# A two-layer mixture-of-experts kernel: the experts' output bias moves from 8-row products into VectorE's gated product, and the adapter step's operands are zero-filled to 128 rows

## The chip, the cores and the metric

The kernel runs on one core of a Trainium2 chip. The metric is the device time in microseconds; smaller is better. The engines are called by the names of the profile: PE is TensorE's products, PEld its weight loads, DVE is VectorE, ACT ScalarE, POOL GpSimd, and SP the engine that issues most DMAs. A name with a q behind it (SPq) is an engine's queue.

## The reference, cut to what matters

```python
# layer 0: 8 experts over all 2048 tokens, every expert weighted by a gate (many gates are zero)
h = gelu_tanh(einsum('bld,ehd->bleh', x, w1) + b1)
y = einsum('bleh,edh->blde', h, w2) + b2.T            # b2: one vector of 128 per expert
out = einsum('blde,ble->bld', y, gates)
# layer 1: an adapter per sample, chosen by its language id, then a norm ...
h = relu(einsum('bsh,bha->bsa', x, W1[lang]) + b1[lang])
adapted = einsum('bsa,bah->bsh', h, W2[lang]) + b2[lang]
x1 = layernorm(x + adapted) * gamma[lang] + beta[lang]
# ... and 8 experts, of which each token takes two
out_e = einsum('eblh,ehd->ebld', gelu(einsum('bld,edh->eblh', layernorm(x1), w1) + b1), w2) + b2[:, None, None, :]
x = x + einsum('ble,ebld->bld', cw, out_e) + x1
```

There are N = 2048 tokens of width 128, in four groups g of 512. An expert has 512 hidden units, in four chunks of 128.

## The kernel before

**Tiling.** A "dense unit" is one expert's chunk of 128 hidden units for one group of 512 tokens. On PE it takes three products for the first matrix (L573 to L575, a high and a low part of each operand), a Gelu on ACT (L643), and one f32 product for the second matrix (L620), which the profile counts as two. Four units make a step: one expert's output y for one group. There are 32 steps in layer 0. Then come 19 "tiles" of 256 sorted tokens (layer 1 for groups 0 to 2, L550 to L552 and L612 to L614), and last 8 dense steps for group 3 of layer 1.

**Order.** Nothing is scheduled while the program runs. Every piece of work is put into its engine's queue by `at(engine, position, function)`, and the positions are in units of PE's dense work. The table `AT` holds the distances of the small work, and `HURRY` holds those for group 2. An engine runs its queue strictly in this order and waits on semaphores.

**Sums.** Each y is multiplied by its gate row, copied to all 128 partitions (Gs, loaded by SP at L762), on DVE into a ring of three buffers tmp (`gated`, L709). POOL adds tmp into acc (`add`, L738). Terms that do not need a gate are copied from PE's bank to tmp by ACT (`copied`, L725). `terms` lists all of them in order. The first 12 steps of layer 0 are finished before the gates are known, so ACT keeps their y in SBUF (L688).

**Output bias.** The sum over experts of gate times b2 is a product with 8 rows (the experts): `b2_mm`, L1219, with b2f (8x128) as weights and gTb (8x2048, the gates by expert) as the moving operand, one product for each group of layer 0 and one for group 3 of layer 1. For groups 0 to 2 of layer 1 the same product opens the bank in which the sorted results come together (`moe`, L1756), and 128-row products L1760 follow it.

**Adapter step.** `mid(g)` runs once for each group, when the sum of layer 0 for it is complete. Its first PE work is `pe_h` (L1237); ACT writes the relu to hTs, whose row 33 is all ones for the bias. Then `pe_xa` does, for each of four blocks of 128 tokens, a product with the identity (L1258: x itself) and one with hTs and cw2 (L1259: 32 rows and the bias row) into the same bank. DVE takes its statistics (L1267), and the norm, the logits (L1371), the choice of experts and, for groups 0 to 2, the scatter of the tokens into sorted order (POOL, L1637) follow. The tiles can't start before the last of these scatters.

**Bank ring.** Small products share PSUM banks 6 and 7; a plan by position (`misc`) gives each its bank and the semaphore that it waits for.

Of the kernel before, what the change touches and what calls it, by code (L numbers as in the profile page):

```python
# [12 lines left out]
ALU = mybir.AluOpType  # L13
# [5 lines left out]
NG = 4  # L19
# [110 lines left out]
def build_adaln_ffn(nc, t, out):  # L130
# [19 lines left out]
    with ExitStack() as ctx:  # L150
# [65 lines left out]
        b2f = [sb(f"b2f{i}", [E, D]) for i in range(2)]  # L216
# [53 lines left out]
        cw2 = sb("cw2", [A + 1, B, D])  # L270
        fgb = sb("fgb", [D, 2])
        hTs = sb("hTs", [A + 1, 512])
# [67 lines left out]
        s_gtb = [sem(f"s_gtb{i}") for i in range(1 + NG)]  # L340
# [26 lines left out]
        b_b2 = sem("b_b2")  # L367
# [88 lines left out]
        def group_of(kind, v):  # L456
            return STEPS[v][2] if kind == "y" else (v if kind in ("x2", "moe") else v[1])

        def layer_of(kind, v):
            return STEPS[v][0] if kind == "y" else (1 if kind in ("x2", "moe") else v[0])  # L460
# [21 lines left out]
        for g in range(NG):  # L482
            misc.append((4 * ND + 6 + 5 * g + 0.35, ("b2", (0, g)), in_tmp(where[("b2", (0, g))])))
# [15 lines left out]
        misc.append((UD + 8.35, ("b2", (1, 3)), in_tmp(where[("b2", (1, 3))])))  # L499
# [195 lines left out]
        def gated(i, v):  # L695
            def fn(dve):
# [12 lines left out]
                dve.tensor_tensor(o, src, Gs[:, j % NGS, :], ALU.mult).then_inc(s_tmp, 1)  # L709
            return fn  # L710

        def copied(i, kind, v):
            def fn(act):
                if i >= NTMP:
                    act.wait_ge(s_acc, i - NTMP + 1)
                if kind == "b2":
                    act.wait_ge(b_b2, [("b2", x) for _, k, x in terms if k == "b2"].index(("b2", v)) + 1)
                    src = bank[mb[("b2", v)][0]]
                elif kind == "moe":
# [186 lines left out]
        def sp_later(sp):  # L906
            sp.dma_start(b2f[0][:, :], t["b2_0"]).then_inc(load_sem("b2f0"), 16)
            sp.dma_start(b2f[1][:, :], t["b2_1"]).then_inc(load_sem("b2f1"), 16)
# [13 lines left out]
            sp.wait_ge(p_no, B)  # L922
            for b in range(B):
# [3 lines left out]
                sp.dma_start(cw2[:, b, :], t["cw2"][bass.ds(r, 1), :, :].rearrange("a p c -> p (a c)")).then_inc(s0, 16)  # L927
# [281 lines left out]

        b2_order = [v for _, k, v in terms if k == "b2"]  # L1210

        def b2_mm(v):
# [704 lines left out]
```

## Time and profile before

| | us |
|---|---|
| median of 3 runs | 413.64 (412.56 to 415.41) |
| time of the profiled execution | 413.44 |
| span of its trace | 411.6 |
| PE busy | 384.4 (93%) |
| DVE busy | 194.7 (47%) |
| ACT busy | 213.2 (52%) |
| POOL busy | 174.1 (42%) |

The span runs from the first to the last instruction in the trace; 1.8 us of the execution's own time lie outside it. Busy time of the matmuls is modelled and overlaps; the distance between starts in the chain of waits is the better measure of what one costs.

The trace falls into stretches. Up to 50 us lie the attention pooling and the first weights. From 50 to 224 us PE runs dense units of layer 0, while the threshold of the gates is found on DVE and, from 128 us, the gated terms are summed. From 224 to 276 us follow the adapter step of group 2 and the scatters, beside the last dense units of layer 0. From 276 to 345 us are the tiles, with the adapter step of group 3 among them. From 352 us come the last dense units, and the sorted results of groups 0 to 2 are added.

### The profile page before, as it was taken

The numbers are of one execution on the slowest core, as the hardware profiler recorded it, in microseconds if no ns is written. First come the engines' busy times: TensorE is split into PE (matmuls) and PEld (weight loads), VectorE is DVE, ScalarE is ACT, GpSimd is POOL, SyncE is SP. The second block draws the span as 40 slices with busy tenths as digits, with TensorE's granted clock in tenths as the row PEclk, the third lists the DMA queues.
The fourth block names the chain that finished last, engine by engine and source line by source line (L and its number), as shares of the span: only waits on it lengthen the run. The fifth ranks groups of instructions, "written<-read, shape, count | busy, mean of one in ns | idle before, by whom it ended". The sixth has DMA issues, their size and how long they took to land.

```text
span 411.6 us, 6974 instructions
## 1 busy us (share of the span) xinstructions
PE 384.4 (93%) x2005; PEld 245.4 (60%) x2005; DVE 194.7 (47%) x679; ACT 213.2 (52%) x373; POOL 174.1 (42%) x172
## 2 busy tenths in 40 slices
PE   6789999999999999999999988969999899899993
PEld 5667765565555555666666655537888787344441
DVE  0556324455512241463774866315799983223521
ACT  1064345454554343366567446438698997334430
POOL 3055200000003876742478166752175330488833
PEclk9699999999999999999999899989999999999998
DMA  7758696220007633222354011121244427242211
GB/s 225 220 155 272 182 390 254 57 54 2 0 6 190 147 90 114 83 76 78 84 154 125 25 37 38 51 84 30 79 132 143 116 72 185 56 81 54 63 35 51
DMA packets 49296, 44.15 MB, mean 107 GB/s; under 512 B 7244, under 2 KB 40420, under 8 KB 49132
## 3 DMA queue, kind: packets, MB, share of 16 engines
q1 hardware_dynamic: 45240, 37.77, 31.8%
q0 software_dynamic: 2688, 5.25, 4.4%
q10 hardware_dynamic: 1332, 0.69, 0.7%
q8 instruction: 18, 0.29, 0.3%
q14 instruction: 18, 0.15, 0.1%
HBM read 32.02 MB, written 11.67 MB: 106 GB/s over the span
## 4 chain that ended last, share of the span: by engine, by line
PE 71%; DVE 8%; issue 5%; POOL 5%; DMA 4%; SPq 2%; ACT 1%; ACTq 1%; POOLq 0%; DVEq 0%
PE bank L620 28%; PE bank L573 8%; PE bank L574 7%; PE bank L575 7%; POOL sorted_in L1637 3%; PE bank L987 2%; DMA vm<-in_vm 2%; DVE l L669 2%; PE bank L1259 2%; PE bank L1258 2%; PE bank L937 2%; DMA sorted_out<-yo 1%; SPq L762 1%; PE bank L1219 1%; PE bank L550 1%
## 5 line engine op out<-in xcount | busy, mean ns | idle before, releaser
L643 ACT ACTIVATE h<-bank,b1f 128x512 f32<-128x512 f32 x160 | 109.7, 687 | 141.3 <-PE bank L620 138.6
L620 PE MATMUL bank<-h,w 128*128 128x512 f32 x320 | 164.7, 598 | 1.9 <-DVE yo L1700 1.9
L738 POOL TENSOR_TENSOR acc<-acc,tmp 128x512 f32<-128x512 f32 x52 | 70.9, 1364 | 112.5 <-DVE tmp L709 104.3
L573 PE MATMUL bank<-xh,wh 128*128 128x512 f32 x128 | 87.0, 680 | 0.0
L620 PEld LDWEIGHTS bank<-h,w 128*128 128x128 f32 x320 | 60.3, 191 | 18.9 <-DVE yo L1700 2.4
L709 DVE TENSOR_TENSOR tmp<-bank,Gs 128x512 f32<-128x512 f32 x28 | 19.3, 688 | 67.7 <-PE bank L620 67.6
L574 PE MATMUL bank<-xl,wh 128*128 128x512 f32 x128 | 51.3, 401 | 0.0
L575 PE MATMUL bank<-xh,wl 128*128 128x512 f32 x128 | 50.9, 398 | 0.0
L573 PEld LDWEIGHTS bank<-xh,wh 128*128 128x128 f32 x128 | 24.4, 190 | 30.5 <-issue 17.5
L574 PEld LDWEIGHTS bank<-xl,wh 128*128 128x128 f32 x128 | 24.5, 192 | 19.0 <-issue 19.0
L637 ACT ACTIVATE h<-bank,b1f 128x256 f32<-128x256 f32 x76 | 31.6, 478 | 5.3 <-PE bank L552 4.0
L1728 POOL DMA_INDIRECT wh<-sorted_out,idx x24 | 23.0, 957 | 23.6 <-DMA sorted_out<-yo 17.5
L1694 POOL TENSOR_TENSOR xtl<-wraw,xth 128x256 f16<-128x256 f32 x19 | 15.9, 838 | 38.5 <-DVE xth L1690 38.5
L612 PE MATMUL bank<-first,h 128*128 x152 | 27.9, 219 | 1.7 <-DVE l L669 1.5
L575 PEld LDWEIGHTS bank<-xh,wl 128*128 128x128 f32 x128 | 24.2, 189 | 5.9
L669 DVE SCALAR_TENSOR_TENSOR l<-h 128x512 f16<-128x512 f32 x38 | 27.2, 721 | 0.7 <-ACT h L656 0.5
L613 PE MATMUL bank<-first,h 128*128 x152 | 27.5, 220 | 0.0
L614 PE MATMUL bank<-first,l 128*128 x152 | 27.4, 219 | 0.0
L1637 POOL DMA_INDIRECT sorted_in<-n2A,idx x24 | 24.3, 1012 | 7.0 <-issue 5.8
L550 PE MATMUL bank<-xth,first 128*128 128x256 f16 x76 | 21.2, 279 | 1.8 <-POOL xtl L1694 0.9
L551 PE MATMUL bank<-xtl,first 128*128 128x256 f16 x76 | 21.1, 277 | 0.0
L552 PE MATMUL bank<-xth,first 128*128 128x256 f16 x76 | 21.0, 277 | 0.0
(203 smaller groups left out, 564.5 us busy)
## 6 DMA issues: line engine op xcount, KB each, us to landing
Gs<-gates SPq DMA_DIRECT2D x40, 256.0 KB, 5.2
sorted_in<-zer SPq DMA_DIRECT2D x14, 448.0 KB, 4.4
w<-in_w SPq DMA_DIRECT2D x16, 256.0 KB, 3.8
wraw<-in_w SPq DMA_DIRECT2D x8, 512.0 KB, 3.7
wraw<-sorted_in SPq DMA_DIRECT2D x19, 128.0 KB, 2.2
sorted_out<-yo SPq DMA_DIRECT2D x19, 128.0 KB, 1.9
wh<-in_w POOLq DMA_DIRECT2D x8, 256.0 KB, 4.1
wraw<-in_w SPq DMA_DIRECT2D x8, 256.0 KB, 3.3
```

What stands on the lines that cost most here:

```text
L573: pe.matmul(o[:, :], w_h, a, start=True, stop=False)
L574: pe.matmul(o[:, :], w_h, b_, start=False, stop=False)
L575: pe.matmul(o[:, :], w_l, a, start=False, stop=True).then_inc(s_m1, 1)
L612: pe.matmul(oo, a, w_h, start=(c == 0 and k == 0 and z == 0), stop=False, skip_group_check=True)
L613: pe.matmul(oo, a, w_l, start=False, stop=False, skip_group_check=True)
L614: last = pe.matmul(oo, b_, w_h, start=False, stop=(c == 1 and k == 1), skip_group_check=True)
L620: pe.matmul(o[:, :], w2[:, e, c * 128:c * 128 + 128], h32[:, u % NH, :], start=(c == 0), stop=(c == 3))\
L637: last = act.activation(h32[:, u % NH, k * TS:k * TS + TS], bank[u % 4][:, k * TS:k * TS + TS], ACT.Gelu, bias=b1f[1][:, 2 * c + k:2 * c + ...
L643: act.activation(h32[:, u % NH, :], bank[u % 4][:, :], ACT.Gelu if layer else ACT.Gelu_apprx_tanh, bias=b1f[layer][:, e * 4 + c:e * 4 + c ...
L669: dve.scalar_tensor_tensor(l16[:, u % NH, :], h32[:, u % NH, :], HS, h16[:, u % NH, :], ALU.mult, ALU.subtract).then_inc(s_lo, 1)
L738: pool.tensor_tensor(a, a, tmp[:, i % NTMP, :], ALU.add).then_inc(s_acc, 1)
L1637: pool.indirect_dma_start(scx, bass.IndirectOffsetOnAxis(idx[:, k, i:i + 1], 0), n2A[:, i, :], None)\
```

## The change

In layer 0 and for group 3 of layer 1, b2 is added to y on DVE before the gate multiplies it: one scalar_tensor_tensor, (y + b2T[:, e]) * Gs, in place of the product of two tensors. So b2T, the bias with the width on the partitions, is loaded for both layers (128x8 each). The five b2 products, their five copies on ACT and their five additions on POOL go. Two kinds of transfer go with them: the copy of all layer 0 gates into gTb, and group 3's of layer 1. The `moe` products for groups 0 to 2 stay as they are.

cw2 and hTs become tensors of 128 rows. POOL fills both with zeros at the start of the program, and the 33 rows that count are written over them. L1259's product has 128 rows from then on, with the same result.

```diff
-        b2f = [sb(f"b2f{i}", [E, D]) for i in range(2)]
+        b2f = sb("b2f", [E, D])
+        b2T = [sb(f"b2T{i}", [D, E]) for i in range(2)]
...
-        cw2 = sb("cw2", [A + 1, B, D])
+        cw2 = sb("cw2", [128, B, D])
...
-        hTs = sb("hTs", [A + 1, 512])
+        hTs = sb("hTs", [128, 512])
...
         for g in range(NG):
-            terms.append((4 * ND + 7 + 5 * g + 0.4, "b2", (0, g)))
             terms.append((M0[g] + after("x2a", g), "x2", g))
-        terms.append((UD + 8.4, "b2", (1, 3)))
...
         for g in range(NG):
-            misc.append((4 * ND + 6 + 5 * g + 0.35, ("b2", (0, g)), in_tmp(where[("b2", (0, g))])))
...
-        misc.append((UD + 8.35, ("b2", (1, 3)), in_tmp(where[("b2", (1, 3))])))
...
-                dve.tensor_tensor(o, src, Gs[:, j % NGS, :], ALU.mult).then_inc(s_tmp, 1)
+                layer, e, _, _ = STEPS[v]
+                if v == 0 or v == NS0:
+                    dve.wait_ge(ld[f"b2T{layer}"], 16)
+                dve.scalar_tensor_tensor(o, src, b2T[layer][:, e:e + 1], Gs[:, j % NGS, :], ALU.add, ALU.mult)\
+                    .then_inc(s_tmp, 1)
...
         def sp_later(sp):
-            sp.dma_start(b2f[0][:, :], t["b2_0"]).then_inc(load_sem("b2f0"), 16)
-            sp.dma_start(b2f[1][:, :], t["b2_1"]).then_inc(load_sem("b2f1"), 16)
+            for i in range(2):
+                sp.dma_start(b2T[i][:, :], t[f"b2T_{i}"]).then_inc(load_sem(f"b2T{i}"), 16)
+            sp.dma_start(b2f[:, :], t["b2_1"]).then_inc(load_sem("b2f1"), 16)
...
             sp.dma_start(scr[0].rearrange("t e p -> (t e) p"), gT0[:, :]).then_inc(s_scr, 16)
-            sp.wait_ge(s_scr, 16)
-            sp.dma_start(gTb[:, :].rearrange("e (t p) -> e t p", p=128), scr[0].rearrange("t e p -> e t p"))\
-                .then_inc(s_gtb[0], 16)
...
-                pe.wait_ge(s_gtb[0] if layer == 0 else s_gtb[1 + g], 16)
-                pe.matmul(o[:, :], b2f[layer][:, :], gTb[:, g * 512:g * 512 + 512], start=True, stop=True)\
-                    .then_inc(b_b2, 1)
...
             pool.wait_ge(t_zm, 3)
+            pool.memset(cw2[:, :, :], 0.0).then_inc(m_one, 1)
+            pool.memset(hTs[:, :], 0.0).then_inc(m_one, 1)
+            pool.wait_ge(m_one, 2)
             pool.memset(hTs[A:A + 1, :], 1.0).then_inc(m_one, 1)
-            pool.wait_ge(m_one, 1)
+            pool.wait_ge(m_one, 3)
```

On PE the first of the five 8-row products stood between dense units 54 and 55 of layer 0. Before (h and w are the second matrix's operands, xh, xl, wh, wl the first's):

```order
L575 MATMUL bank<-xh,wl 128x512
L620 MATMUL bank<-h,w 128x512
L1219 MATMUL bank<-gTb,b2f 128x512
L573 MATMUL bank<-xh,wh 128x512
L574 MATMUL bank<-xl,wh 128x512
```

In the changed kernel the same place on PE, with its own line numbers (L571 for L575, L616 for L620, L569 for L573, L570 for L574):

```order
L571 MATMUL bank<-xh,wl 128x512
L616 MATMUL bank<-h,w 128x512
L569 MATMUL bank<-xh,wh 128x512
L570 MATMUL bank<-xl,wh 128x512
L571 MATMUL bank<-xh,wl 128x512
```

The product is gone and nothing has taken its place; the other four went in the same way. The adapter step of each group keeps its order on PE, and only the rows of its operands change (the view gives shapes of results, so the new rows read like the old). On SP, behind the store of layer 0's gates (gates<-gT), this stood before:

```order
L1201 DMA gates<-gT 128x128 [waits b_ev]
L1203 DMA gTb<-gates 8x16x128 [waits s_scr0]
L762 DMA Gs<-gates 128x4x128 [waits s_scr0] x6
L762 DMA Gs<-gates 128x4x128 [waits s_tmp,s_scr0] x18
L807 DMA wraw<-in_w 128x1024 [waits s_w16]
```

and this stands now:

```order
L1200 DMA gates<-gT 128x128 [waits b_ev]
L759 DMA Gs<-gates 128x4x128 [waits s_scr0] x6
L759 DMA Gs<-gates 128x4x128 [waits s_tmp,s_scr0] x18
L804 DMA wraw<-in_w 128x1024 [waits s_w16]
L759 DMA Gs<-gates 128x4x128 [waits s_tmp,s_scr0]
```

The copy into gTb is gone, and the gate rows follow the store at once.

## Rows read from the trace of the kernel before

**Rows 1.** The page, part 1: busy us (share of the span) xinstructions.

```profile
PE 384.4 (93%) x2005; PEld 245.4 (60%) x2005; DVE 194.7 (47%) x679; ACT 213.2 (52%) x373; POOL 174.1 (42%) x172
```

**Rows 2.** Busy time by stretch; columns: stretch, length, five engines, granted clock, DMA share, GB/s.

```profile
127.00:157.00 30.00, 30.00 (x89) 15.94 (x88) 10.88 (x15) 12.46 (x19) 22.38 (x16) 1.00 0.60 153
157.00:224.00 67.00, 66.94 (x248) 40.86 (x248) 33.63 (x105) 37.54 (x57) 40.04 (x38) 1.00 0.36 100
...
228.00:231.40 3.40, 3.40 (x8) 1.98 (x7) 3.19 (x31) 0.80 (x1) 1.27 (x2) 0.50 0.03 10
...
276.00:279.10 3.10, 3.10 (x10) 1.50 (x11) 0.00 (x0) 0.00 (x0) 1.89 (x2) 0.50 0.35 95
279.10:345.00 65.90, 63.35 (x719) 53.25 (x718) 53.83 (x141) 58.72 (x130) 24.50 (x26) 1.00 0.35 100
...
352.00:404.00 52.00, 52.00 (x177) 24.04 (x176) 16.91 (x32) 21.30 (x32) 36.46 (x35) 1.00 0.24 56
```

**Rows 3.** Chain of waits around the first 8-row product: start, us, what.

```profile
127.18 1.05 PE bank L1219 x2
128.23 0.44 PE bank L573
...
129.99 0.23 PE bank L573
```

**Rows 4.** Chain of waits, adapter products of group 0.

```profile
161.50 0.46 PE bank L1258 x2
161.96 0.42 PE bank L1259 x2
...
164.46 0.42 PE bank L1259 x2
164.88 0.43 PE bank L573
```

**Rows 5.** Timeline of the weight loads (PEld): start, us, engine, line, what [idle before].

```profile
127.11 0.29 PEld L1219 LDWEIGHTS bank<-gTb,b2f 8*128 8x128 f32 x2 [0.76 <-issue]
...
161.89 0.29 PEld L1259 LDWEIGHTS bank<-cw,hTs 33*128 33x128 f32 x2
...
164.92 0.19 PEld L574 LDWEIGHTS bank<-xl,wh 128*128 128x128 f32 x1
```

**Rows 6.** Chain of waits, other small f32 products, and group 3's 8-row product.

```profile
33.10 0.89 PE bank L987 x8
...
358.96 1.05 PE bank L1219 x2
360.01 0.32 PE bank L573
...
367.19 0.42 PE bank L1760 x2
...
370.62 0.22 PE bank L1760 x2
```

**Rows 7.** Timeline of DVE from the adapter products of group 2 on.

```profile
226.38 0.38 DVE L1406 TENSOR_TENSOR pr<-ex,c 128x32 f32<-128x32 f32 x1
227.65 0.89 DVE L1267 BATCH_NORM_STATS2 st<-bank 128x6 f32<-128x128 f32 x4 [0.89 <-PE bank L1259]
...
233.56 1.23 DVE L841 SCALAR_TENSOR_TENSOR first<-wraw,first 128x1024 f16<-128x1024 f32 x1 [0.26 <-ACT first L833]
```

**Rows 8.** Timeline of PE: its idle time ahead of group 2's transposes.

```profile
242.67 0.63 PE L1348 MATMUL bank<-ident,n2A 128*128 128x128 f32 x4 [1.74 <-DVE n2A L1333]
```

**Rows 9.** The page, part 5: count, busy, mean ns of one, idle before.

```profile
L709 DVE TENSOR_TENSOR tmp<-bank,Gs 128x512 f32<-128x512 f32 x28 | 19.3, 688 | 67.7 <-PE bank L620 67.6
...
L669 DVE SCALAR_TENSOR_TENSOR l<-h 128x512 f16<-128x512 f32 x38 | 27.2, 721 | 0.7 <-ACT h L656 0.5
```

**Rows 10.** Timeline of POOL: fills at the start, and an addition between the scatters.

```profile
0.73 0.95 POOL L1770 MEMSET xh<- 128x1024 f32 x1 [0.29 <-POOLq L1905]
...
6.62 0.72 POOL L814 DMA_DIRECT2D wh<-in_w  x1 [2.95 <-DMA acc<-in_xT]
...
251.35 1.27 POOL L738 TENSOR_TENSOR acc<-acc,tmp 128x512 f32<-128x512 f32 x1 [1.57 <-DVE tmp L709]
```

More of the change, by code:

```diff
@@ L339, in build_adaln_ffn @@
         s_scr1 = [sem(f"s_scr1_{g}") for g in range(NG)]
-        s_gtb = [sem(f"s_gtb{i}") for i in range(1 + NG)]
+        s_gtb = [sem(f"s_gtb{i}") for i in range(GA)]
         s_out = sem("s_out")
@@ L366, in build_adaln_ffn @@
         b_ev = sem("b_ev")
-        b_b2 = sem("b_b2")
         m_h = sem("m_h")
@@ L456, in group_of @@
         def group_of(kind, v):
-            return STEPS[v][2] if kind == "y" else (v if kind in ("x2", "moe") else v[1])
+            return STEPS[v][2] if kind == "y" else v
         def layer_of(kind, v):
-            return STEPS[v][0] if kind == "y" else (1 if kind in ("x2", "moe") else v[0])
+            return STEPS[v][0] if kind == "y" else 1
         done0 = {g: max(i for i, (_, k, v) in enumerate(terms) if group_of(k, v) == g and layer_of(k, v) == 0) + 1
@@ L715, in fn @@
                     act.wait_ge(s_acc, i - NTMP + 1)
[L716 to L719, printed above, removed]
+                if kind == "moe":
                     act.wait_ge(t_moe, 4 * v + 4)
@@ L922, in sp_later @@
             sp.wait_ge(p_no, B)
+            sp.wait_ge(m_one, 3)
             for b in range(B):
@@ L926, in sp_later @@
                 sp.dma_start(cb1[:, b:b + 1], t["cb1"][bass.ds(r, 1), :].rearrange("a p -> p a")).then_inc(s0, 16)
-                sp.dma_start(cw2[:, b, :], t["cw2"][bass.ds(r, 1), :, :].rearrange("a p c -> p (a c)")).then_inc(s0, 16)
+                sp.dma_start(cw2[0:A + 1, b, :], t["cw2"][bass.ds(r, 1), :, :].rearrange("a p c -> p (a c)")).then_inc(s0, 16)
                 sp.dma_start(gbc[:, b, :], t["gbc"][bass.ds(r, 1), :].to_broadcast([128, 2 * D])).then_inc(s0, 16)
@@ L1208, in build_adaln_ffn @@
         at("sp", PG + 1, gates0_out)
-        b2_order = [v for _, k, v in terms if k == "b2"]
-        def b2_mm(v):
-            layer, g = v
-            def fn(pe):
-                o = misc_bank(pe, ("b2", v))
-                pe.wait_ge(ld[f"b2f{layer}"], 16)
-                pe.wait_ge(s_gtb[0] if layer == 0 else s_gtb[1 + g], 16)
-                pe.matmul(o[:, :], b2f[layer][:, :], gTb[:, g * 512:g * 512 + 512], start=True, stop=True)\
-                    .then_inc(b_b2, 1)
-            return fn
-        for v in b2_order:
-            at("pe", mpos[("b2", v)], b2_mm(v))
         def mid(g):
@@ L1244, in act_h @@
                     act.wait_ge(ld["lang"], 16 * 4 * B)
+                    act.wait_ge(m_one, 3)
                 else:
@@ L1253, in pe_xa @@
                 o = misc_bank(pe, ("xa", g))
-                pe.wait_ge(m_one, 1)
+                pe.wait_ge(m_one, 3)
                 pe.wait_ge(m_hs, 2 * g + 2)
@@ L1504, in mid @@
             at("sp", m + after("cT", g) + 0.5, sp_gates)
-            at("sp", m + after("cT", g) + 3.0, sp_gtb)
+            if g < GA:
+                at("sp", m + after("cT", g) + 3.0, sp_gtb)
         for g in range(NG):
@@ L1750, in fn @@
                     o = misc_bank(pe, ("moe", g))
-                    pe.wait_ge(s_gtb[1 + g], 16)
+                    pe.wait_ge(s_gtb[g], 16)
                     pe.wait_ge(ld["b2f1"], 16)
@@ L1755, in fn @@
                 if i % 4 == 0:
-                    pe.matmul(o[:, :], b2f[1][:, :], gTb[:, g * 512:g * 512 + 512], start=True, stop=False,
+                    pe.matmul(o[:, :], b2f[:, :], gTb[:, g * 512:g * 512 + 512], start=True, stop=False,
                               skip_group_check=True)
@@ L1890 @@
                                  .reshape(128, E, 4 * D)], axis=2)),
-        "b2_0": i["L0_ffn_b2"],
+        "b2T_0": c(i["L0_ffn_b2"].T),
+        "b2T_1": c(i["L1_ffn_b2"].T),
         "cw1": i["L1_cond_W1"],
```

3 lines of the change are left out of this document (1 added, 2 removed).

## The prediction

> **What bounds the kernel now.** I read the page's busy shares first: PE is busy for 384.4 of 411.6 us, no other engine for more than 213.2 [rows 1]. That is an average, so the busy times by stretch came next. From 127 to 157 us and from 157 to 224 us PE is busy for 30.00 of 30.00 and 66.94 of 67.00 us, and from 352 to 404 us for 52.00 of 52.00 [rows 2]. There every microsecond taken from PE's queue moves what follows. Then I read the chain of waits and the timelines at the places that the change touches, and in the stretches where PE does not lead: group 2's adapter step with the scatters (224 to 276 us), where the chain goes through DVE and POOL and PE at one place waits 1.74 us for n2A [rows 8], and the tiles, where PE is busy for 63.35 of 65.90 us, but ACT for 58.72 and DVE for 53.83 [rows 2], so that the three share the bound. Last, the granted clock: it is 0.50 of full speed (the lower level, 1.2 GHz) from 228.0 to 231.4 us, right after group 2's adapter products, and again from 276.0 to 279.1 us, after PE had been mostly idle; elsewhere in these stretches it is 1.00 [rows 2].
>
> **The change, part by part.**
>
> *The 8-row products.* One of them stands in the chain with 1.05 us, and the L573 behind it takes 0.44 us where its neighbour takes 0.23 [rows 3]. The weight loads say why: L1219's own load starts with its product, after 0.76 us in which the loader stood still [rows 5], and the next 128-row load isn't made under it either. So one costs 1.05 + 0.21 = 1.26 us of PE. Four of them lie between 127 and 157 us, where PE is never idle [rows 2]: 4 x 1.26 = 5.04 us. The fifth, in the last stretch, costs 1.05 + (0.32 - 0.22, the neighbours there) = 1.15 us [rows 6]. All leave the path: 6.19 us.
>
> *The adapter products.* In group 0's step the eight products take 0.46 + 7 x 0.42 = 3.4 us, first and last of the seven shown [rows 4], and the L573 behind them 0.43 where 0.23 is usual: 3.6 us in all. So after the change I expect 0.46 for the first, whose load still starts behind its wait, and 7 x 0.22 for the rest, 2.0 us: 1.6 us less for each group.
> - Groups 0 and 1 lie between 157 and 224 us, bound by PE: 2 x 1.6 = 3.2 us.
> - In group 2 the gain passes to DVE. But DVE has been idle for only 0.89 us when it takes the statistics [rows 7]; if they are ready sooner, it still has L1406 to finish. So 0.89 us get through. PE also stops being a hindrance for the weight conversion L841, which waited 0.26 us [rows 7]. Together 1.15 us. From there to the tiles DVE and POOL lead, and PE's further gain only adds to the 1.74 us that it waits for n2A. POOL's wait of 1.57 us for a gated term [rows 10] comes behind that wait of PE's, so it moves with the chain and doesn't shrink.
> - Group 3's products lie among the tiles. 1.6 us of PE are worth their whole size if DVE and ACT catch up, nothing if they are full. PE is the busiest of the three [rows 2], and they are idle while it does these products; I take 1.3 us of 1.6.
>
> A rule of the Trainium skill speaks against this part. "TensorE: Matmul & The Clock Gate", in the sections on loading the stationary operand and on packing small matmuls, says that a load depends on its columns alone, that one product with 32 rows takes the same time as one with 128, and that a load overlaps a running product only when its row group differs. By this, filling up with zeros would give nothing: the sum would be 6.19 us in place of 11.7, and the time 407.3 us. L1760 at 0.22 and at 0.42 us [rows 6] contradicts it as far as this case shows anything before the change: what decides is whether neighbours have the same rows.
>
> *DVE's product.* 40 of them become scalar_tensor_tensor. Before, the tensor product from a bank takes 688 ns; a scalar_tensor_tensor of 128x512 takes 721 ns on other operands [rows 9]. I take the 33 ns: it adds 1.3 us to DVE where it waits for PE (67.7 us of idle time ahead of L709 [rows 9]), and some 0.1 us to the path, in the three products that lie on it (two in group 2's step, one at the very end). From below it is nothing. From above I bound it by L841, the same operation on twice the columns, at 1.23 us [rows 7]: 0.54 us each, 1.6 us in those three, and still hidden elsewhere.
>
> *Copies and additions.* Five copies on ACT and five additions on POOL go. POOL is busy for 22.38 of 30.00 us where four lie, and waits for others there [rows 2], so I count nothing. One margin shrinks: the adapter step of group 0 waits for the last addition of its layer 0 sum, and PE gets there sooner. But the terms ahead of it are fewer too, 11 for 14, and the term that decides comes from PE itself. If POOL is late, PE waits for one addition, 1.27 us [rows 10].
>
> *Fills at the start.* Two more fills on POOL: 128x1024 by L1770 takes 0.95 us [rows 10], and half of that for hTs, so about 1.5 us. They lie ahead of L814, which waited 2.95 us for the input [rows 10]. Hidden; without the cover 1.5 us would delay the first weights.
>
> *DMAs.* SP issues one small load more long before it is needed, and two copies to gTb fewer. The gate rows of layer 0 may come a little sooner; PE doesn't wait for them. Nothing.
>
> *The clock.* Of the lower level between 228.0 and 231.4 us about 1.7 us are PE's loss, but it falls ahead of the wait for n2A, so its end is worth little beyond the 0.26 us counted. The fall at 276.0 us, 3.10 us long, costs about 1.6 us on the path. The scatters and the idle time before it stay, so I keep it.
>
> **Sum.** 5.04 + 3.2 + 1.15 + 1.3 + 1.15 - 0.1 = 11.7 us. Against the profiled execution's 413.44 us this gives 401.7 us. It lies 0.20 us under the median of the runs shown, so the forecast holds for both.
>
> **The rivals.**
> - *Zero rows are no help.* The adapter products stay at 0.42 us each, since a load of the identity's or cw2's partner is never made under the product before it, whatever the rows. Then L1760's 0.42 comes from its own wait for data and not from the 8 rows ahead. Then only the 8-row products count, 6.19 us: 413.44 - 6.19 = 407.3 us. Chance 0.12. It is also where the Trainium skill's rule above would put the time.
> - *The gain stops at the scatters.* DVE, with the choice of experts for group 1 in its queue, and POOL between 224 and 276 us might be later than the chain shows: slow DVE operations beside POOL's, additions that wait for PE. If 4 of the 8.2 us won before are given back there, the time is 405.7 us. Against it: everything in the stretch starts from PE's products. Chance 0.10.
> - *The second fall of the clock also goes*, because the tiles start at another moment. Then 1.6 us more: 400.1 us. This is a matter of chance; it is part of the forecast's own range, as is one more fall on the path, 403.4 us.
> - *Slower than before.* PE's wait for n2A grows from 1.74 us by the 1.6 us of products and by up to 1.7 us of clock, less 1.15: to almost 4 us. If the clock falls there and stays low for the dense units up to 271 us, each microsecond at 0.50 costs half of one. The gain of 11.7 us is used up after 23 us at the lower level; with all 31 us from 240 to 271 at it, the time is 401.7 + 15.5 = 417.2 us. Against it: both falls in rows 2 ended within 3.4 us once PE was dense again. Chance 0.03.
>
> **How the numbers follow.** Forecast 0.75, with 399.5 to 404 us as its own range; gain stopped 0.10; no help from zeros 0.12; slower 0.03. I predict 401.7 us. The range should hold 8 in 10: it starts at 399, below the case without a second fall, and reaches to 407.5 to take in both cases of a smaller gain. One per cent, about 4.1 us, is what a measurement of this kernel can tell from no change. Faster by over 1% (under 409.5 us) are all cases but the last and a rest of mishaps that I can't name: 0.91. Within 1%: 0.06. Slower: 0.03.
>
> **What would show it.** In the changed profile the distance between the L620 products should be regular from 127 to 157 us. The adapter products should take about 2 us for a group, all of 0.22 us but the first, with weight loads under the products. DVE's idle time ahead of group 2's statistics should be gone. PE should be idle for over 3 us ahead of group 2's transposes. The tiles should start about 9.4 us sooner than at 276 us, and DVE's gated product should take 690 to 720 ns. Adapter products that still take 0.42 us would prove the sum wrong by 5.6 us; a start of the tiles that moved by less than 7 us would show that the scatters' chain has a bound of its own.

## The result, and the profile after

The changed kernel takes 405.58 us in the median of its four executions (399.35 to 408.75), and the kernel before, run beside it, 414.52. Two of the four, 406.62 and 408.75 us, lie over 1.5% above the fastest and count as slow, and the ratio of 0.9719, with an interval of 0.9661 to 0.9777, is that of the fast executions alone, 404.54 and 399.35 us: faster by 2.2 to 3.4%. Predicted were 401.7 us in a range of 399.0 to 407.5. Run once more beside the first experiments, the same kernel gave 405.22 us in six executions (ratio 0.9767, 0.9718 to 0.9816). Before stands at 414.12 there. By the medians of all executions the gain is 8.9 us both times, by the ratios 11.6 and 9.6; 11.7 were forecast. The execution that was profiled is the slowest of the four, 408.75 us with a span of 406.4; I therefore read its trace together with the second one, of 406.0 us (label after_again), and rest nothing on what only the first one shows.

Part 1 of the page and, from part 5, DVE's gated product in its form from a bank, beside [rows 1] and [rows 9]:

```profile
PE 375.8 (92%) x1995; PEld 242.4 (60%) x1995; DVE 194.0 (48%) x679; ACT 210.2 (52%) x368; POOL 171.2 (42%) x169
...
L708 DVE SCALAR_TENSOR_TENSOR tmp<-bank,b2T,Gs 128x512 f32<-128x512 f32 x28 | 21.0, 749 | 68.1 <-PE bank L616 65.0
```

PE has ten products fewer (each 8-row product counts as two) and is busy for 8.6 us less. DVE's product costs 61 ns more, not 33.

Busy time by stretch of the changed kernel (columns as in [rows 2]):

```profile
127.00:157.00 30.00, 30.00 (x97) 17.60 (x96) 14.23 (x15) 12.38 (x18) 20.71 (x14) 1.00 0.71 168
157.00:224.00 67.00, 66.47 (x269) 42.33 (x268) 36.73 (x132) 39.80 (x59) 41.36 (x40) 1.00 0.38 102
...
237.50:240.90 3.40, 3.40 (x7) 1.98 (x6) 1.06 (x2) 1.29 (x2) 2.78 (x3) 0.50 0.08 24
271.60:275.00 3.40, 3.40 (x12) 1.73 (x11) 0.00 (x1) 0.47 (x1) 1.90 (x2) 0.51 0.30 87
...
346.70:350.10 3.40, 3.40 (x7) 1.20 (x6) 0.00 (x0) 0.69 (x1) 1.26 (x2) 0.50 0.26 77
```

From 127 to 157 us PE now does 97 products where it did 89. The adapter stretch is still full of PE, but for about half a microsecond. The fall of the clock at 228.0 us is gone and one at 237.5 us has come; the fall ahead of the tiles stayed (271.6 us, before 276.0).

The adapter products of group 0 in the timeline of PE (start, us, engine, line, what), and under them one of their weight loads (engine PEld), beside [rows 4] and [rows 5]:

```profile
158.64 0.46 PE L1238 MATMUL bank<-ident,acc 128*128 128x128 f32 x2
158.94 0.39 PE L1239 MATMUL bank<-cw,hTs 128*128 128x128 f32 x2
159.16 0.39 PE L1238 MATMUL bank<-ident,acc 128*128 128x128 f32 x2
...
160.28 0.39 PE L1239 MATMUL bank<-cw,hTs 128*128 128x128 f32 x2
160.42 0.48 PE L569 MATMUL bank<-xh,wh 128*128 128x512 f32 x1
```

```profile
158.83 0.30 PEld L1239 LDWEIGHTS bank<-cw,hTs 128*128 128x128 f32 x2
```

The 0.39 us is a product's whole length in the pipeline; what it costs is the distance to the next start, 0.22 us, where it was 0.42. The load starts at 158.83, under the product of 158.64, where it used to start with its own product. The eight take 158.64 to 160.42, 1.8 us.

Now the places where the gain was lost. In the timelines of PE, DVE and POOL (in brackets the idle time before, and what ended it):

```profile
213.77 1.02 PE L1216 MATMUL bank<-acc,cw 128*32 128x256 f32 x4 [0.46 <-POOL acc L735]
...
230.28 0.63 PE L1321 MATMUL bank<-ident,x 128*128 128x128 f32 x4 [1.68 <-DVE x L1297]
...
236.60 0.63 PE L1328 MATMUL bank<-ident,n2A 128*128 128x128 f32 x4 [2.42 <-DVE n2A L1313]
```

```profile
220.91 1.04 DVE L1386 TENSOR_TENSOR pr<-ex,c 128x32 f32<-128x32 f32 x1
221.88 0.88 DVE L1247 BATCH_NORM_STATS2 st<-bank 128x6 f32<-128x128 f32 x4
...
233.45 3.00 DVE L1313 TENSOR_SCALAR n2A<-x,mv,rs 128x128 f32<-128x128 f32 x4 [1.46 <-POOL rs L1266]
```

```profile
220.59 1.31 POOL L735 TENSOR_TENSOR acc<-acc,tmp 128x512 f32<-128x512 f32 x1
...
233.40 2.72 POOL L735 TENSOR_TENSOR acc<-acc,tmp 128x512 f32<-128x512 f32 x2
...
246.93 1.28 POOL L735 TENSOR_TENSOR acc<-acc,tmp 128x512 f32<-128x512 f32 x1 [3.16 <-DVE tmp L708]
```

And of the kernel before, DVE's operation pr<-ex,c (L1406, now L1386) for group 0, and POOL's addition that ran when group 2's began [rows 7]:

```profile
194.89 0.19 DVE L1406 TENSOR_TENSOR pr<-ex,c 128x32 f32<-128x32 f32 x1
...
225.43 1.27 POOL L738 TENSOR_TENSOR acc<-acc,tmp 128x512 f32<-128x512 f32 x1
```

Four things stand here. Group 2's adapter step waits 0.46 us for POOL's last addition; before, it did not wait. The statistics L1247 have lost their idle time, but L1386 ahead of them takes 1.04 us where it took 0.38 [rows 7]. Alone it takes 0.19. Beside an addition it ends 0.05 to 0.07 us behind the addition's end, in all 28 cases of the fourteen profiles of this document. So what changed is how late the addition comes: before, it had begun 0.95 us ahead of this operation, now 0.32. PE waits 1.68 us for DVE's x, where it did not wait before, and then 2.42 us for n2A where it waited 1.74 [rows 8]; right behind it the clock falls, and PE's term for POOL comes so late that the addition between the scatters waits 3.16 us, not 1.57 [rows 10]. And n2A itself, four operations of 128x128, takes 3.00 us, as long as POOL's two additions beside it.

**Where the kernels stand.** For each profile I took the start of the same product (the third first-matrix product of a dense unit or a tile) and subtracted its start in the trace before. "Start" is that difference at unit 20 (71.20 us before); the other columns are net of it, so that they show only what came between. Last come the falls of the granted clock to 0.50 in that profile, 3.4 us each (they leave out a first one, at about 12 us, and one at the very end, which all have).

| label | start | unit 70 | unit 102 | unit 103 | tile 0 | unit 159 | falls at, us |
|---|---|---|---|---|---|---|---|
| before, at us | 71.20 | 155.88 | 218.03 | 220.77 | 276.32 | 399.69 | 228.0, 275.8 |
| after | 2.13 | -5.00 | -8.09 | -7.61 | -6.83 | -7.47 | 32.7, 237.5, 271.6, 346.7 |
| after_again | 1.74 | -5.00 | -8.06 | -7.58 | -6.89 | -9.64 | 32.2, 237.0, 271.2 |
| bias_only | 2.18 | -4.99 | -3.38 | -2.91 | -1.82 | -3.08 | 33.3, 193.7, 241.5, 275.6 |
| pad_only | 1.48 | 0.01 | -3.09 | -3.11 | -3.09 | -4.30 | 32.4, 240.6, 274.7 |
| rows64 | -0.26 | -5.00 | -3.45 | -2.97 | -3.24 | -4.74 | 190.2, 272.1 |
| fill_nT | 1.31 | -5.00 | -8.09 | -7.61 | -8.50 | -12.59 | 31.8 |
| fill_all | -0.80 | -5.00 | -8.10 | -7.61 | -7.19 | -10.09 | 268.5 |
| add_early | -0.82 | -4.99 | -8.09 | -8.10 | -7.28 | -9.85 | 234.0, 268.2 |
| no_bias_add | -0.43 | -5.00 | -8.09 | -8.11 | -7.95 | -11.37 | 232.9, 267.0 |
| n2_clear | 0.98 | -4.99 | -8.09 | -7.61 | -10.37 | -12.92 | 31.9, 267.4 |
| moe128 | -0.02 | -5.00 | -8.09 | -7.61 | -8.39 | -12.23 | 268.1 |
| best | -0.20 | -5.00 | -8.09 | -8.11 | -10.83 | -16.48 | none |
| best_nofill | -0.84 | -5.00 | -8.10 | -8.11 | -10.65 | -14.21 | 337.9 |

### The profile page after: what moved, and what is told of

Same layout as the page of the kernel before. It is cut to its first block and busy times, and to the rows that moved or that the text cites. A ratio compares the mean times of both kernels' runs of the same rounds, so it can differ in the third digit from the quotient of the medians.

```text
span 406.4 us, 6929 instructions
## 1 busy us (share of the span) xinstructions
PE 375.8 (92%) x1995; PEld 242.4 (60%) x1995; DVE 194.0 (48%) x679; ACT 210.2 (52%) x368; POOL 171.2 (42%) x169
## 5 line engine op out<-in xcount | busy, mean ns | idle before, releaser
L616 PE MATMUL bank<-h,w 128*128 128x512 f32 x320 | 165.8, 602 | 1.9 <-DVE yo L1680 1.9
L735 POOL TENSOR_TENSOR acc<-acc,tmp 128x512 f32<-128x512 f32 x47 | 65.3, 1389 | 116.5 <-DVE tmp L708 112.9
L569 PE MATMUL bank<-xh,wh 128*128 128x512 f32 x128 | 88.2, 689 | 1.0 <-ACT h L639 0.9
L616 PEld LDWEIGHTS bank<-h,w 128*128 128x128 f32 x320 | 60.6, 192 | 19.1 <-DVE yo L1680 2.4
L708 DVE SCALAR_TENSOR_TENSOR tmp<-bank,b2T,Gs 128x512 f32<-128x512 f32 x28 | 21.0, 749 | 68.1 <-PE bank L616 65.0
L570 PE MATMUL bank<-xl,wh 128*128 128x512 f32 x128 | 51.5, 402 | 0.0
L571 PE MATMUL bank<-xh,wl 128*128 128x512 f32 x128 | 51.1, 399 | 0.0
L569 PEld LDWEIGHTS bank<-xh,wh 128*128 128x128 f32 x128 | 24.7, 193 | 30.0 <-issue 18.0
L570 PEld LDWEIGHTS bank<-xl,wh 128*128 128x128 f32 x128 | 24.7, 193 | 19.7 <-issue 19.7
L1708 POOL DMA_INDIRECT wh<-sorted_out,idx x24 | 23.1, 961 | 23.8 <-DMA sorted_out<-yo 17.5
L1617 POOL DMA_INDIRECT sorted_in<-n2A,idx x24 | 25.4, 1057 | 7.0 <-issue 5.8
L571 PEld LDWEIGHTS bank<-xh,wl 128*128 128x128 f32 x128 | 24.3, 190 | 5.9
L818 POOL TENSOR_TENSOR wl<-wraw,wh 128x512 fp32r<-128x512 f32 x8 | 10.2, 1275 | 25.9 <-DMA w<-in_w 21.7
```

Of the source, the lines that this page charges most:

```text
L569: pe.matmul(o[:, :], w_h, a, start=True, stop=False)
L570: pe.matmul(o[:, :], w_h, b_, start=False, stop=False)
L571: pe.matmul(o[:, :], w_l, a, start=False, stop=True).then_inc(s_m1, 1)
L616: pe.matmul(o[:, :], w2[:, e, c * 128:c * 128 + 128], h32[:, u % NH, :], start=(c == 0), stop=(c == 3))\
L735: pool.tensor_tensor(a, a, tmp[:, i % NTMP, :], ALU.add).then_inc(s_acc, 1)
L1617: pool.indirect_dma_start(scx, bass.IndirectOffsetOnAxis(idx[:, k, i:i + 1], 0), n2A[:, i, :], None)\
```

## The experiments

### One part of the change alone

bias_only: the bias in DVE's product, but the adapter operands with their 33 rows.

```diff
-        cw2 = sb("cw2", [128, B, D])
+        cw2 = sb("cw2", [A + 1, B, D])
...
-        hTs = sb("hTs", [128, 512])
+        hTs = sb("hTs", [A + 1, 512])
...
-            pool.memset(cw2[:, :, :], 0.0).then_inc(m_one, 1)
-            pool.memset(hTs[:, :], 0.0).then_inc(m_one, 1)
-            pool.wait_ge(m_one, 2)
```

> The changed kernel with cw2 and hTs at 33 rows again, so only the bias half of the change. Theory (the two halves are worth 6.2 and 5.6 us of PE and add up): the five 8-row products are gone, adapter products alternate 0.42 us each as before, time 6.2 us under the kernel before, about 407.5. Rival (8-row products were hidden and all the gain is the zero rows): no change, 413 to 414.

Measured: 410.82 us, ratio 0.9901 (0.9860 to 0.9943), so 4.1 us by the ratio, where 6.2 were expected. In the table its four products bring 4.99 us by unit 70. Then it loses: 1.6 us up to unit 102, the wait for POOL's addition up to unit 103, and more in the scatter stretch. The windows of two of its falls (bias_only, columns as before):

```profile
193.70:197.10 3.40, 3.40 (x8) 1.97 (x7) 3.19 (x32) 0.79 (x1) 1.27 (x2) 0.50 0.62 182
241.50:244.90 3.40, 3.24 (x10) 2.47 (x10) 2.08 (x7) 0.78 (x1) 2.24 (x2) 0.50 0.02 5
```

The first lies right behind group 1's adapter products, which still have 33 rows, as the fall at 228.0 us lay right behind group 2's in the kernel before. So the removed products are worth what was said, and the fall behind the 33-row products takes 1.6 us of it back.

pad_only: the kernel before with the zero rows alone (the same two sizes of 128, their fills and the wait for them).

> The kernel before with cw2 and hTs zero-filled to 128 rows and nothing else. Theory: adapter products 0.22 us each but the first, 1.5 to 1.6 us of PE per group, 4 to 5.6 us in all less what the scatter stretch swallows: 409 us. Rival (the step's length is set by something else): products at 0.22 but time within 1 us of before.

Measured: 409.04 us, ratio 0.9858 (0.9795 to 0.9921), so 5.9 us by the ratio (2.7 us in its profile, which took 410.71 and starts 1.48 late). The table has 3.09 us at unit 102, that is 1.54 for each of groups 0 and 1. Two rows of its PE timeline:

```profile
163.29 0.39 PE L1261 MATMUL bank<-cw,hTs 128*128 128x128 f32 x2
163.51 0.39 PE L1260 MATMUL bank<-ident,acc 128*128 128x128 f32 x2
```

Again 0.22 us apart. Zero rows help; the rival that says they don't has fallen. By the ratios the two parts alone make 10.0 us, and both together 9.6 and 11.6; with intervals of 2 us and more to each side they add up as far as this can be told.

rows64: the whole change, but with 64 rows.

```diff
-        cw2 = sb("cw2", [128, B, D])
+        cw2 = sb("cw2", [64, B, D])
...
-        hTs = sb("hTs", [128, 512])
+        hTs = sb("hTs", [64, 512])
```

> The changed kernel with cw2 and hTs zero-filled to 64 rows only. If it is enough that the rows of two neighbouring products are the same in 32-row strips or that they are many, 64 rows would be as good as 128; if only equal rows with the identity product's 128 count, L1239 and L1238 stay at 0.42 us each and the time is that of bias_only, 4 to 5 us above the changed kernel.

Measured: 409.70 us, ratio 0.9884 (0.9805 to 0.9962), from two executions. PE, then PEld, in the timeline of rows64:

```profile
156.64 0.49 PE L1239 MATMUL bank<-cw,hTs 64*128 64x128 f32 x2
157.06 0.49 PE L1238 MATMUL bank<-ident,acc 128*128 128x128 f32 x2
```

```profile
156.64 0.29 PEld L1239 LDWEIGHTS bank<-cw,hTs 64*128 64x128 f32 x2
157.06 0.30 PEld L1238 LDWEIGHTS bank<-ident,acc 128*128 128x128 f32 x2
```

With 64 rows the distance is 0.42 us as with 33, and each load starts with its own product. The 128-row product behind a 64-row one pays too, and between the two passes of a 64-row product, which have equal rows, nothing is paid: with 0.20 us there as well it would take 0.6 us. So it is not the number of rows that costs, but that the products beside them have 128. Row counts between 64 and 128 were not tried. "TensorEngine Tiling (Array Packing)" of the Trainium skill says in its key properties that a change of the tiling mode drains the engine. That products of 64 or 33 rows run in another mode than those of 128 no run shows; the 0.20 us for each change between them would fit it. And the rule that the prediction weighed, from Part 3 of "TensorE: Matmul & The Clock Gate" of the Trainium skill (a load goes under a running product only when the row group differs), is contradicted by this case as it stands: between products of the same 128 rows the load does go under, and they are 0.22 us apart.

after_again: the changed kernel, unaltered, beside these three.

> The changed kernel unaltered, timed again in five rounds and profiled again. Theory (the profiled execution had four stretches at the lower clock, two more than the kernel before, each worth 1.6 us, and the rest of the loss against the prediction is a POOL addition ahead of group 2 and a slower scatter chain): median near 403, and the execution's time goes with the number of low-clock stretches. Rival (the change itself makes the scatter chain slower by more): the tile stretch starts less than 5 us sooner even where the clock doesn't fall ahead of it.

Measured: 405.22 us (403.82 to 406.08), ratio 0.9767; the expected median near 403 was not reached. Its profile repeats the changed kernel's within 0.06 us net of the start up to the tiles, with the same fall behind the wait for n2A. The fall at 346.7 us is missing; it belongs to one execution.

### What became of the gain in the scatter stretch

fill_nT: 24 small bf16 products on ones, whose result nobody reads, ahead of group 2's n2A transposes.

```diff
+        def filler(pe, o, n):
+            for _ in range(n):
+                pe.matmul(o[:, 0:128], onesb[:, :], onesb[:, :], start=True, stop=True)
...
+                if g == GA - 1:
+                    filler(pe, o, 24)
```

> The changed kernel with 24 extra bf16 products of 128 columns (results unused) on PE ahead of group 2's transposes of n2A, where PE stood idle for 2.4 us and the clock fell right behind. They take about as long as the idle time. Theory (that fall costs 1.6 us of the scatter chain, because POOL's addition between the scatters waits for a gated term of slowed units): no low clock near 237 us, POOL's wait for that term back from 3.2 to about 1.6 us, tiles 1.6 us sooner than in the changed kernel. Rival (the fall was hidden by the scatters): clock full, tiles start within 0.4 us of the changed kernel's, time the same.

Measured: 402.35 us, ratio 0.9688 (0.9641 to 0.9735). Windows, PE and POOL of fill_nT:

```profile
230.00:240.00 10.00, 9.01 (x56) 6.06 (x55) 6.19 (x18) 3.93 (x7) 6.75 (x7) 1.00 0.16 38
```

```profile
233.17 1.50 PE L941 MATMUL bank<-onesb 128*128 128x128 bf16 x24
...
235.66 0.66 PE L1335 MATMUL bank<-ident,n2A 128*128 128x128 f32 x4 [0.99 <-DVE n2A L1318]
```

```profile
244.44 1.27 POOL L735 TENSOR_TENSOR acc<-acc,tmp 128x512 f32<-128x512 f32 x1 [1.52 <-DVE tmp L708]
```

The clock stays at 1.00, and POOL's wait between the scatters is 1.52 us, as before the change, in place of 3.16. Other profiles say the same without fillers: rows64 and moe128 have PE's full wait of 2.42 us but no fall, and there POOL waits 1.58 and 1.55 us, while in the six profiles with the fall it waits 3.09 to 3.20. So it is the clock and not PE's wait that makes POOL wait longer. At tile 0 the table has 8.50 us against 6.86. So a fall behind the wait for n2A costs 1.6 us. Whether it is PE's idle time that brings it takes all the profiles: eight of them have the wait of 2.35 to 2.42 us (after, after_again, bias_only, pad_only, rows64, add_early, no_bias_add, moe128), and in six of these the clock falls within 0.9 us of its end; in rows64 and moe128 it does not. With the wait filled or shortened (fill_nT, fill_all, n2_clear, best, best_nofill) it falls in none of five. The idle time makes the fall likely, not certain.

fill_all: the same, with 3 x 7 such products ahead of the first tile and 18 ahead of the first second-matrix product of the last stretch.

```diff
+                    if v == 0 and c == 0:
+                        pe.wait_ge(s_g, u - 3)
+                        filler(pe, o, 7)
...
+                if i in (1, 2):
+                    filler(pe, o, 7)
...
+                if kind == "dense" and v == NS0 and c == 0:
+                    pe.wait_ge(m_cE, 4)
+                    filler(pe, bank[mb[("moe", 0)][0]], 18)
```

> As fill_nT, with extra products also in PE's idle times ahead of the first tile (three times 7) and ahead of the first L616 of the last dense stretch (18). Theory: no fall of the clock after 230 us; against the changed kernel 1.6 us from the place above, 1.6 us from the first tile, and nothing or 1.7 us at the last stretch by whether the changed kernel had a fall there; 3 to 4 us less in all, about 401. Rival (falls come from elsewhere and only move): as many falls as in the changed kernel.

Measured: 402.93 us, ratio 0.9706 (0.9667 to 0.9745): not to be told from fill_nT, and not the 401 that were expected. The fall at the first tile came although that place was filled too (268.5 us), and was missing in fill_nT, where it was not. Tile 0 also starts 1.3 us later than in fill_nT, about what 21 products of some 0.06 us take (24 took 1.50). So fillers there cost their own time and don't decide the fall, and I can't say what does.

add_early: one of POOL's additions (the term of step 23) goes into its queue one scatter sooner.

```diff
-            at("pool", pos + AT["add"], add(i, kind, v))
+            at("pool", pos + (0.55 if (kind, v) == ("y", 23) else AT["add"]), add(i, kind, v))
```

> The changed kernel with one pair of POOL instructions swapped: the addition of the last layer-0 term of group 2 comes one scatter sooner. Theory (PE's 0.45 us of idle time ahead of group 2's L1216 comes from POOL reaching this addition late, behind scatters; the margin was used up by the bias half): the idle time goes and everything up to the tiles is 0.45 us sooner. Rival (PE waits there for the term itself, that is for its own product): idle time unchanged.

Measured: 401.69 us, ratio 0.9681 (0.9638 to 0.9724). In its PE timeline group 2's step starts without idle time:

```profile
210.29 1.05 PE L1216 MATMUL bank<-acc,cw 128*32 128x256 f32 x4
```

The table shows the 0.48 us between units 102 and 103 won back, and still there at tile 0 (7.28 against 6.83). The rest of what lies between its median and after_again's, 3.5 us, is not its doing: its profile starts 2.56 us sooner at unit 20, before anything that it changes.

no_bias_add: DVE's product without the bias. It leaves out b2 of layer 0 and of group 3 in layer 1.

```diff
-                dve.scalar_tensor_tensor(o, src, b2T[layer][:, e:e + 1], Gs[:, j % NGS, :], ALU.add, ALU.mult)\
+                dve.tensor_tensor(o, src, Gs[:, j % NGS, :], ALU.mult)\
```

> The changed kernel with tensor_tensor (y * Gs) again in place of scalar_tensor_tensor, which leaves out the output bias b2 in layer 0 and for group 3 of layer 1. Theory (DVE's longer product is hidden but for three of them): 690 ns for one in place of 750, total within 0.3 us of the changed kernel. Rival (the longer product lies on the path in the stretches where PE leads): 40 times 0.06, 2.4 us sooner.

Measured: 403.04 us, ratio 0.9724 (0.9668 to 0.9780), from two executions, not to be told apart from the changed kernel's. But it too has no wait between units 102 and 103. POOL, then DVE, of no_bias_add:

```profile
206.40 0.96 POOL L1617 DMA_INDIRECT sorted_in<-n2A,idx  x1 [0.30 <-issue]
207.66 0.96 POOL L1617 DMA_INDIRECT sorted_in<-n2A,idx  x1 [0.31 <-issue]
208.64 1.29 POOL L735 TENSOR_TENSOR acc<-acc,tmp 128x512 f32<-128x512 f32 x1
```

```profile
206.39 1.26 DVE L838 SCALAR_TENSOR_TENSOR first<-wraw,first 128x1024 f16<-128x1024 f32 x1
```

and the same of the changed kernel:

```profile
209.07 1.98 POOL L1617 DMA_INDIRECT sorted_in<-n2A,idx  x1 [0.30 <-issue]
211.36 0.96 POOL L1617 DMA_INDIRECT sorted_in<-n2A,idx  x1 [0.30 <-issue]
212.34 1.28 POOL L735 TENSOR_TENSOR acc<-acc,tmp 128x512 f32<-128x512 f32 x1
```

```profile
209.01 1.22 DVE L838 SCALAR_TENSOR_TENSOR first<-wraw,first 128x1024 f16<-128x1024 f32 x1
```

With the bias in it, the product ahead of L838 is 60 ns longer. L838 then starts 0.06 us before the scatter's issue, not with it, and the issue takes 1.98 us in place of 0.96. So a microsecond on POOL hangs on some tens of nanoseconds on DVE. The other profiles bear it out. In the three kernels without the bias in DVE's product (before, pad_only, no_bias_add) the two start within 0.01 us and the issue takes 0.96 us; in the eleven with it L838 starts 0.04 to 0.09 us sooner, the issue takes 1.96 to 2.01 us, and its end comes 0.82 to 0.84 us behind L838's. No run moved L838 alone, so that it is L838 that holds the issue up rests on this order in time.

The microsecond is lost twice behind it. no_bias_add has no wait at unit 103, and its L1386 takes 0.40 us, where the changed kernel's takes 1.04, since POOL's addition ahead of it comes sooner again. With the same two falls of the clock it stands at 7.95 us at tile 0, the changed kernel at 6.89 (after_again).

### Removing the causes

n2_clear: POOL's two additions beside n2A are moved, one ahead of it, one behind it. The second edit makes the addition of group 2's own rows wait until n2A is written.

```diff
-            at("pool", pos + AT["add"], add(i, kind, v))
+            at("pool", pos + (0.1 if (kind, v) == ("y", 25) else AT["add"]), add(i, kind, v))
...
                     pool.wait_ge(m_xa, v + 1)
+                    if v == GA - 1:
+                        pool.wait_ge(m_n2, GA)
```

> The changed kernel with two POOL additions moved out of DVE's n2A of group 2: one goes ahead of the second rstd of group 2, into POOL's 7.3 us of idle time, and the x2 term's waits until n2A is written. Theory (the four n2A operations take 3.0 us instead of 1.1 because POOL adds beside them; this was so before the change too, and it is what stands between PE's gain and the scatters): n2A 1.1 us in all, PE's idle time ahead of its transposes 0.5 us instead of 2.4, no fall of the clock behind it, tiles 1.9 us sooner by the chain and up to 1.6 more by the clock: 400 to 402. Rival (n2A is slow for another reason, its operands for one): still 3.0 us and no gain.

Measured: 400.13 us, ratio 0.9630 (0.9571 to 0.9689). DVE, PE and POOL of n2_clear:

```profile
232.33 1.12 DVE L1315 TENSOR_SCALAR n2A<-x,mv,rs 128x128 f32<-128x128 f32 x4 [1.52 <-POOL rs L1268]
```

```profile
233.59 0.63 PE L1330 MATMUL bank<-ident,n2A 128*128 128x128 f32 x4 [0.60 <-DVE n2A L1315]
```

```profile
242.31 1.28 POOL L737 TENSOR_TENSOR acc<-acc,tmp 128x512 f32<-128x512 f32 x1 [0.80 <-DVE tmp L708]
```

n2A takes 1.12 us, not 3.00; PE waits 0.60, not 2.42; the clock doesn't fall there; POOL waits 0.80, not 3.16. At tile 0 the table has 10.37 us against 6.89, so 3.5 us: this is the largest single loss of the stretch, and part of it was there before the change (n2A took as long in the kernel before, 3.02 us, with PE waiting 1.74 us [rows 8]). "GPSIMD Engine Reference" of the Trainium skill, in its table of specifications, says that POOL's interfaces to SBUF are shared with VectorE, and that they contend when VectorE's instruction is in a two-port mode or has two inputs in SBUF. 3.00 us beside the additions and 1.12 without them agree with a contention; in which mode n2A runs no run shows.

moe128: the last 8-row products, those that open the bank of the sorted results, get 120 zero rows: POOL fills both tensors with zeros, and the 8 rows that count are loaded behind that.

```diff
...
-        b2f = sb("b2f", [E, D])
+        b2f = sb("b2f", [128, D])
+        gTz = sb("gTz", [128, GA * 512])
...
-                    pe.matmul(o[:, :], b2f[:, :], gTb[:, g * 512:g * 512 + 512], start=True, stop=False,
+                    pe.matmul(o[:, :], b2f[:, :], gTz[:, g * 512:g * 512 + 512], start=True, stop=False,
```

> The changed kernel with the three 8-row bias products of the sorted groups (L1756 of before) filled up with zeros to 128 rows as well. Theory (rows that differ from the neighbours' cost an 8-row product 0.19 us and the one behind it 0.20 us): 0.86 and 0.22 us in place of 1.05 and 0.42, 3 times 0.4 = 1.2 us less at the end. Rival (the 1.05 us belong to the f32 product's waits, not to its rows): 1.05 as before, no gain.

Measured: 401.77 us, ratio 0.9693 (0.9622 to 0.9764). The chain of waits, moe128 and then the changed kernel:

```profile
355.06 0.86 PE bank L1745 x2
355.92 0.22 PE bank L1749 x2
```

```profile
360.79 1.05 PE bank L1736 x2
361.84 0.42 PE bank L1740 x2
```

1.08 us in place of 1.47, 0.39 less for this one of the three. The same result over the same 512 columns is cheaper with 128 rows than with 8. Units 134 to 159 gain 2.33 us against before, where the changed kernel gains 1.15: 1.18 us for the three. The rest of the difference between its profile and after_again's is the start (1.76 us sooner) and the fall at 237 us, which is missing here, and neither is the edit's doing.

best: add_early, n2_clear and moe128 together, and 8 fillers ahead of the transposes. best_nofill: the same without the fillers.

> The changed kernel with four edits: the swap of add_early, the moves of n2_clear, the 128 rows of moe128, and 8 extra products ahead of group 2's transposes. Theory, from the parts: 0.5 + 1.9 + 1.6 + 1.2 us under the changed kernel, 399 to 400, and under both kernels. Rival (the parts share one gain, since the additions moved in n2_clear hold up the terms behind them): no better than the best single part.

> The same without the 8 extra products. Theory (with n2A at 1.1 us PE's idle time there is too short for the clock to fall): within 0.3 us of the version with them. Rival (the fall needs the extra products to be kept away): 1.6 us slower.

Measured: 396.91 us (396.17 to 398.50), ratio 0.9577 (0.9530 to 0.9624), and 397.43 us, ratio 0.9576 (0.9509 to 0.9643). Both beat both kernels, and the 399 to 400 us that were expected: 17.5 us under the kernel before, and some 8 under the changed one's two medians. The fillers bring nothing that can be measured once PE's idle time is short. Part 1 of the page of best:

```profile
PE 369.1 (93%) x2003; PEld 240.6 (61%) x2003; DVE 194.0 (49%) x679; ACT 209.8 (53%) x368; POOL 171.5 (43%) x171
```

## Why the prediction was right, and where its sum was off

The sum was 11.7 us. The profile of after_again, the less disturbed of the two, took 406.0 us against 413.44: 7.4 us. Term by term:

- **The 8-row products, 4 x 1.26 = 5.04.** Right: 5.00 at unit 70, in all twelve profiles that have this edit. The fifth, 1.15 us, is seen too: units 134 to 159 gain 1.15 us against before in both profiles of the changed kernel, and nothing in pad_only's.
- **The adapter products of groups 0 and 1, 3.2.** Right: 3.09 at unit 102. All products are 0.22 us apart but the first; where 2.0 us were forecast for the eight, 1.8 were measured, and the saving came out as 1.54 for each group where it was put at 1.6.
- **Group 3's, 1.3 of 1.6.** Right: tile 0 to tile 12 gains 1.20 us in both profiles. The step itself, between tiles 4 and 5, gains 1.46; 0.25 was lost between tiles 0 and 1.
- **Group 2's, 1.15.** Here the step failed. Between units 102 and tile 0 nothing was to be lost, and 1.15 us won. The table has 8.06 and then 6.89: 1.2 us lost instead, 2.35 us short of the sum. Three things make it up, by their single sizes 2.7; where the 0.4 between goes isn't shown. First, 0.48 us at unit 103 for POOL's late addition: the prediction looked at this margin for group 0 alone, where the terms ahead are fewer, and not for group 2, where POOL's scatters stand in the same queue. Second, of the 0.89 us of DVE's idle time 0.66 are eaten by L1386, which ends only when POOL's addition does. Both come from the one late issue on POOL, and no_bias_add, without it, wins back 1.06 of their 1.14 us. Third, 1.6 us for the fall behind n2A, with fill_nT and moe128 as the profiles without it (8.50 and 8.39 at tile 0). With it POOL's wait of 1.57 us, which by the prediction only moves with the chain, grew to 3.16. The prediction had named that mechanism, PE's longer idle time there and the clock behind it, but only as the start of a rare case that costs 15 us; short as it is, one fall of 3.4 us, it is the usual case, six times in eight. It had put PE's idle time ahead of the transposes at over 3 us; it is 4.1, but in two pieces, 1.68 for x and 2.42 for n2A. The 1.4 us that the loss of the fall at 228 us gives back (units 105 to 106) does not help, as forecast: PE only waits longer.
- **DVE's product, -0.1.** The row chosen was 721 ns, and it took 749. On its own term this is nothing; through L838 and the scatter's issue it decides about the first two losses above, 1.1 us, and this path the prediction did not have.
- **What no term had: the start.** Both profiles of the changed kernel are late by 1.7 to 2.1 us at 71 us, and all profiles that show a fall at 31.8 to 33.3 us are late by 1.0 to 2.2, while those without it lie between -0.84 and -0.02. It is not the fills: bias_only has none of them and is late by 2.18, and add_early has them all and is early. I don't know what decides it, nor how often it comes in executions that weren't profiled.

So 11.7 - 2.35 in the scatter stretch - 1.74 at the start = 7.6, and 7.4 were measured in that profile. That the two come so close is partly luck: about 0.4 us won between tile 12 and unit 134 and 0.5 us lost behind unit 159 are in no term either, and they cancel. The medians' 8.9 us and the ratios' 9.6 and 11.6 lie between this and the sum. The time fell inside the range since the terms on PE were right to a tenth or two of a microsecond, but the range reached so far up for other reasons, zeros that do not help and a gain that stops, and took in losses that had no term. The rival "the gain stops at the scatters", with 4 us lost of 8.2 and 405.7 us, names the right place, and its reasons (slow DVE operations beside POOL's, additions late) were the ones at work. Its size was not: 1.2 us were given back there, and the medians lie near its time by the late start as well. I gave it 0.10, which was too little: its counter-argument, that everything there starts from PE's products, overlooks that POOL's queue and n2A don't. The prediction's own test reads that way too: the tiles started 4.7 us sooner, 6.8 net of the start, under the 7 us that it set as the sign of a bound of its own. n2_clear shows that bound.

## What to carry to other kernels

A small product whose rows differ from its neighbours' pays for the load that can't be made ahead, at both its edges; look in the weight loads' timeline whether a load starts with its own product, and fill up with zeros where it does (here 0.42 to 0.22 us, and 1.47 to 1.08 us). Before a gain on the leading engine is counted to the end, walk the queue of every other engine that it will wait for, in each stretch and not at one place only, and read there what runs beside what: a DVE operation that ends just behind one of POOL's, or the other way round, has been held up by it. A wait that grows from 1.7 to 2.4 us can cost twice, once as a wait and once by the clock behind it; moving what makes it long is worth more than filling it.

## What the runs showed of the hardware that was not expected

- n2A, four operations of 128x128 on DVE, takes 3.00 us beside two additions of 128x512 on POOL (2.72 us) and 1.12 us without them. L1386 takes 0.19 us alone; beside an addition it ends 0.05 to 0.07 us behind the addition's end, however long that is, 0.38 to 1.12 us (28 of 28 cases).
- POOL's issue of an indirect DMA takes 0.96 us, but 1.96 to 2.01 when DVE's L838 had begun 0.04 to 0.09 us before it (eleven profiles), and then it ends 0.82 to 0.84 us behind L838; with both started within 0.01 us of each other it took 0.96 (three profiles).
- A 64-row product among 128-row ones is as dear as a 33-row one, 0.42 us.
- The granted clock fell to 0.50 (1.2 GHz) for 3.4 us behind PE's wait of 2.4 us for n2A in six of eight profiles, and not where the wait was 0.99 us behind fillers or 0.60 us. Behind 33- or 64-row products it fell at 193.7 us (bias_only), 190.2 (rows64) and 228.0 (before), so behind three of twelve adapter steps, and behind none of the 44 with 128 rows; but PE counts as busy there, and bias_only had no fall in the place of before's. What decides it is open.
